# Gating of two batches' dense tiles and one addition moved behind the cluster choice in a two-block AdaLN kernel

## The chip, the cores and the metric

The kernel runs on one core of one Trainium2 chip. The metric is the time of one execution on the device, in microseconds (us). Five engines work side by side and meet through semaphores: TensorE (PE in the profile; its weight loads are PEld), VectorE (DVE), ScalarE (ACT), GpSimd (POOL) and SyncE, whose queue (SPq) issues most of the DMAs.

## What is computed

Two transformer blocks run one after the other on x of 4 batches x 512 rows x 512 columns, in float32. The change lies in the feed-forward part of the first block:

```python
mod = (_silu(L0_c) @ L0_wmod).reshape(4, 6, 1, -1)      # sa, ca, ga, sb, cb, gb
h = _layernorm(x) * (1 + ca) + sa
x = x + ga * attention0(h)
h = _layernorm(x) * (1 + cb) + sb
dots = softmax(h @ centroids.T / 0.1)                    # 64 clusters
hits = dots > 0.01
query_sel = any(hits, axis=1)                            # per row
cluster_sel = any(hits, axis=0)                          # over all 2048 rows
row_sel = cluster_sel[assignments]                       # per output column
dense = h @ weight.T + bias
x = x + gb * where(query_sel[:, None] & row_sel[None, :], dense, 0)
```

`cluster_sel` needs the softmax of all four batches. Only after it is known can an output column be taken or left. The second block (attention with 32 query and 8 key heads, and a gated feed-forward) follows and takes about nine tenths of the time.

## The kernel before

The 2048 rows are 16 tiles of 128 rows, four to a batch. The first block is written out by hand: each engine has one list of steps (`first_tensor`, `first_vector`, `first_scalar`, `first_gpsimd`, `first_sync`), run strictly in that order, with waits on semaphores between engines. So a step that waits holds all that stands behind it on its engine.

The steps around the change, by line:

- `add_outputs(b, tiles)` (L946) adds the attention's result in PSUM (PE's `update`, L1212) to x. `statistics2` and `normal2` (L864 to L907) follow, PE transposes the result (L120), ACT modulates it (L125).
- `cluster_logits(b)` (L957, L958) takes the maximum off the logits that PE's `dots` (L1227) left; ACT's `clusters` (L639) takes the exponential; `cluster_hits(b)` (L962 to L967) makes `qsel`, the row flag, and keeps the largest value of each cluster in `top`.
- `columns2(b)` (L1221), the first product of the logits on PE, waits for the `cluster_logits` of the batch before.
- `whole_linear(t)` (L1242, L1245) is PE's dense product of tile t; ACT's `drain` (L643) copies it to `dense`. POOL (L500) makes the low half of each batch's split input for it.
- `gate_dense(b)` (L814) multiplies the four tiles of a batch by `qsel` and the gate row, in place; `add_rows(b)` (L819) adds x. Batches 0 and 1 get this here; batches 2 and 3 go to DRAM and are done later.
- After `cluster_hits(3)`, `topc` (L1063) is reduced, PE transposes it (L1397), DVE makes `topv` and `selb` (L1065 to L1067), and PE spreads the choice over the columns (L1400). That last product raises `chosen` to `ROWS_SPREAD`. DVE waits for it before `select`, and POOL waits for it before it splits the first weights of the second block (L508, L510, eight instructions of 128x512).
- `select(tiles)` (L822) overwrites x by `dense` where the column is taken. It is done for tiles 0 and 1, then 2 and 3, with the second block's statistics (`spread_of`, `variances_2`, `inverse_2`) between; then come `add_rows(1)`, `select` of tiles 4 to 7, and `whole_chunk`/`low_of` (L1108, L1114), which with POOL's `low_chunk` (L530) make the first operands of the second block's products (L2158).
- PE does the dense tiles 12, 13 and 14 after the spreading, then the transposes of batch 0 (L1411), the dense tile 15, the product for a modulation (L1153), the first key product (L2158), the first query product (L2073), and then waits for the normalised batch 1, `normal_second` (L1137), which it transposes (L120).

Of the kernel before, what the change touches and what calls it, by code (L numbers as in the profile page):

```python
# [29 lines left out]
def adaln_two_blocks(nc, x, Wq, bq, Wk, bk, Wv, bv, ffn_w, ffn_b, cent, assign, c0, wmod0,  # L30
# [26 lines left out]
    with ctx:  # L57
# [152 lines left out]
        with l0:  # L210
# [600 lines left out]
            def gate_row(dve, t):  # L811
                dve.wait_ge(rows_sb, 2 * B)
                dve.wait_ge(drained, t + 1)
                return nc.vector.scalar_tensor_tensor(rows(dense, t), rows(dense, t), qsel[:, t:t + 1], gb_rows[:, t // TB, :],  # L814
                                                      ALU.mult, ALU.mult)

            def add_row(t):

                return nc.vector.tensor_tensor(rows(dense, t), rows(dense, t), rows(X, t), ALU.add)  # L819
# [46 lines left out]
            def variances_2(dve, tiles, done):  # L866
                for t in tiles:
                    last = nc.vector.bn_aggr(mv_2[:, t, :], stats[:, t, :])
                link_vector(dve, last)
                v = slice(tiles[0], tiles[-1] + 1)  # L870
                nc.vector.tensor_scalar(mv_2[:, v, 1], mv_2[:, v, 1], EPS, None, ALU.add).then_inc(done, 1)

            def first_vector(dve):
                def link(ins):
                    link_vector(dve, ins)
# [66 lines left out]
                def add_outputs(b, tiles=range(TB)):  # L942
                    for r in tiles:
                        t = TB * b + r
                        dve.wait_ge(upd_ps, t + 1)
                        nc.vector.tensor_tensor(rows(X, t), rows(X, t), ps[:, BANK_U + t % 2, :], ALU.add).then_inc(x1_done, 1)  # L946
# [7 lines left out]
                def cluster_logits(b):  # L954
                    dve.wait_ge(lgps, b + 1)
                    lp = ps[:, BANK_M, 0:TB * NCL].rearrange("p (t k) -> p t k", t=TB)
                    link(nc.vector.tensor_reduce(cred[:, 0], lp, AX.X, ALU.max))  # L957
                    nc.vector.tensor_tensor(lg[:], lp, wide_c(cred[:, 0]), ALU.subtract).then_inc(lg_done, 1)  # L958

                def cluster_hits(b):  # L960
                    dve.wait_ge(exps_done, b + 1)
                    link(nc.vector.tensor_reduce(cred[:, 1], lg[:], AX.X, ALU.add))  # L962
                    link(nc.vector.reciprocal(cred[:, 1], cred[:, 1]))
                    link(nc.vector.tensor_tensor(pr[:], lg[:], wide_c(cred[:, 1]), ALU.mult))
                    link(nc.vector.tensor_reduce(cred[:, 2], pr[:], AX.X, ALU.max))
                    link(nc.vector.tensor_scalar(qsel[:, tiles_of(b)], cred[:, 2], THRESHOLD, None, ALU.is_gt))
                    link(nc.vector.tensor_tensor(top[:], pr[:] if b == 0 else top[:], pr[:], ALU.max))  # L967

                def gate_dense(b):
                    for t in range(TB * b, TB * (b + 1)):  # L970
                        last = gate_row(dve, t)
                    link(last)

                def add_rows(b):
                    for t in range(TB * b, TB * (b + 1)):
                        last = add_row(t)
                    link(last)
# [68 lines left out]
                normal2(2)  # L1046
                cluster_hits(0)
                add_outputs(3, range(2))
                gate_dense(0)
                add_outputs(3, range(2, 3))  # L1050
                cluster_logits(1)
                add_outputs(3, range(3, 4))
# [2 lines left out]
                cluster_hits(1)  # L1055
                one_hot()
                cluster_logits(2)
                gate_dense(1)
                add_rows(0)
                cluster_hits(2)  # L1060
                cluster_logits(3)
                cluster_hits(3)
# [2 lines left out]
                link(nc.vector.tensor_reduce(topv[:, 0:1], ps[0:NCL, BANK_M, 0:P], AX.X, ALU.max))  # L1065
                link(nc.vector.tensor_scalar(topv[:, 1:2], topv[:, 0:1], THRESHOLD, None, ALU.is_gt))
                nc.vector.tensor_scalar(selb[:], ones[:], topv[:, 1:2], None, ALU.mult).then_inc(chosen, 1)  # L1067
                dve.wait_ge(chosen, ROWS_SPREAD)

                def select(tiles):  # L1070
                    for t in tiles:
                        select_row(t, ps[:, BANK_P, :])
                    dve.wait_ge(x2_done, tiles[-1] + 1)
# [6 lines left out]
                def inverse_2(step, tiles):  # L1080
                    v = slice(tiles[0], tiles[-1] + 1)
                    dve.wait_ge(std_2, step + 1)
                    link(nc.vector.reciprocal(rstd_2[:, v], rstd_2[:, v]))
                    nc.vector.scalar_tensor_tensor(shift[:, v], mv_2[:, v, 0], -1.0, rstd_2[:, v], ALU.mult, ALU.mult) \
                        .then_inc(rstd_done, 1)
# [7 lines left out]
                spread_of(HALVES[1])  # L1093
                variances_2(dve, HALVES[1], var_2)
                inverse_2(1, HALVES[1])
                add_rows(1)
                select(range(TB, TB + 2))
                select(range(TB + 2, 2 * TB))
# [334 lines left out]
        with a:  # L1433
# [41 lines left out]
            with at:  # L1475
# [177 lines left out]
                with nc.Block() as block:  # L1653
# [902 lines left out]
                    @block.vector  # L2556
                    def _(dve):
                        first_vector(dve)

                        dve.sem_inc(o_ready, 1)  # L2560
# [358 lines left out]
```

## Time and profile before

| | us |
|---|---|
| median of 3 runs | 1852.1 |
| lowest, highest | 1851.37, 1853.2 |
| the profiled execution | 1854.24 |
| its span on the core | 1852.5 |
| PE busy in it | 1807.5 |
| DVE busy in it | 1283.4 |
| POOL busy in it | 448.1 |

The profiled execution is 2.1 us longer than the median, and 1.7 us of it lie outside the span. A timeline row gives the start, the length of the group, engine, line, operation, output and inputs, shapes and the count; in brackets stands how long the engine had been idle before it, and what released it. First starts and lengths are in us from the span's start. The last length in a row can reach a little into the next row, since the engines pipeline.

### The profile page before, as it was taken

To read this page: it belongs to the slowest core of one execution; us is meant where nothing else is said; L and a number is where in the kernel's file an instruction comes from. 1 tells how busy PE (TensorE), PEld (TensorE's weight loads), DVE (VectorE), ACT (ScalarE), POOL (GpSimd) and SP (SyncE) were. 2 spreads that over 40 slices of the span, in tenths; PEclk is the share of its full clock that TensorE was granted. 3 is DMA by queue.
4 is the path that set the end of the run, shared out by engine and by line. 5 is a ranking of instruction groups with operands and counts; after the bars stand their busy time and mean duration, and the time that the engine had idled before them with its cause. 6 is when DMAs were issued, how large, how long until landed. Compare 5 with 4: busy or idle time off the path is not lost.

```text
span 1852.5 us, 29061 instructions
## 1 busy us (share of the span) xinstructions
PE 1807.5 (98%) x8863; PEld 1508.2 (81%) x8863; DVE 1283.4 (69%) x3032; ACT 1123.1 (61%) x2620; POOL 448.1 (24%) x429
## 2 busy tenths in 40 slices
PE   6998999999999999999999999999999989999999
PEld 4566788888888888888888888888888867888887
DVE  6897677877767676766777777777777785544442
ACT  5755766667667676766666676666666673333331
POOL 2234404041323224041612123140313132010000
PEclk9899999999999999999999999999999999999999
DMA  9026567666766776776776778677777767313010
GB/s 347 2 80 224 157 191 216 203 192 191 204 200 194 211 200 198 205 231 207 214 211 197 208 202 226 191 217 212 197 213 203 210 186 243 109 57 114 27 41 23
DMA packets 239368, 331.25 MB, mean 179 GB/s; under 512 B 26008, under 2 KB 165528, under 8 KB 238880
## 3 DMA queue, kind: packets, MB, share of 16 engines
q1 hardware_dynamic: 238736, 328.93, 59.6%
q8 instruction: 52, 0.85, 0.2%
q10 hardware_dynamic: 528, 1.05, 0.2%
q14 instruction: 52, 0.43, 0.1%
HBM read 200.39 MB, written 129.50 MB: 178 GB/s over the span
## 4 chain that ended last, share of the span: by engine, by line
PE 79%; DVE 7%; DMA 6%; ACT 4%; SPq 2%; issue 2%; DVEq 0%; ACTq 0%
PE ps L2073 23%; PE ps L2139 15%; PE ps L2264 11%; PE ps L2121 9%; PE ps L2106 9%; PE ps L2246 5%; DMA turned_blocks<-tp 4%; ACT probs L2362 2%; PE ps L2125 1%; PE ps L2103 1%; SPq L1779 1%; PE ps L1245 1%; DMA pd<-turned_blocks 1%; DVE pt L2628 1%; DVE stats L864 1%
## 5 line engine op out<-in xcount | busy, mean ns | idle before, releaser
L2073 PE MATMUL ps<-hA,wq 128*128 128x512 f32 x1536 | 385.8, 400 | 0.0
L2139 PE MATMUL ps<-wo,oT 128*128 128x512 f32 x1536 | 367.2, 390 | 3.7 <-issue 2.3
L2139 PEld LDWEIGHTS ps<-wo,oT 128*128 128x128 f32 x1536 | 287.8, 188 | 64.3 <-issue 3.1
L2604 DVE CUSTOM_DVE_ANT_0 ps<-ps,mask 128x512 f32<-128x512 f32 (+3 forms) x512 | 235.8, 523 | 143.5 <-PE ps L2106 142.9
L2381 ACT ACTIVATE pt<-pd 128x1280 fp32r<-128x1280 f32 x128 | 163.0, 1273 | 272.2 <-PE ps L2121 231.3
L2073 PEld LDWEIGHTS ps<-hA,wq 128*128 128x128 f32 x1536 | 279.0, 188 | 56.4 <-issue 0.2
L2362 ACT ACTIVATE probs<-ps,nmax 128x512 f32<-128x512 f32 (+3 forms) x512 | 263.1, 532 | 71.3 <-DVE nmax L2604 71.3
L2370 ACT ACTIVATE probs<-probs,rinv 128x512 f32<-128x512 f32 (+3 forms) x512 | 246.2, 552 | 38.3 <-DVE rinv L2610 38.3
L2121 PE MATMUL ps<-pt,V 128*128 128x512 f32 (+2 forms) x1152 | 253.3, 349 | 11.1 <-DVE pt L2628 10.5
L2121 PEld LDWEIGHTS ps<-pt,V 128*128 128x128 f32 x1152 | 196.2, 190 | 40.3 <-issue 15.3
L2106 PE MATMUL ps<-kT,qT 128*128 128x512 f32 (+2 forms) x1152 | 224.7, 340 | 0.0
L2106 PEld LDWEIGHTS ps<-kT,qT 128*128 128x128 f32 x1152 | 198.9, 189 | 20.2 <-issue 0.2
L2620 DVE STREAM_TRANSPOSE tp<-probs 128x384 f32<-128x384 f32 (+2 forms) x512 | 208.1, 444 | 6.4 <-DMA turned_blocks<-tp 4.7
L2628 DVE TENSOR_TENSOR pt<-pd,pt 128x1280 fp32r<-128x1280 f32 x128 | 193.0, 1508 | 2.5 <-ACT pt L2381 2.5
L2264 PE MATMUL ps<-fT,gw 128*128 128x512 f32 x448 | 110.9, 390 | 1.2 <-DVE dgb L2797 1.2
L2264 PE MATMUL ps<-fT,uw 128*128 128x512 f32 x448 | 110.6, 389 | 0.0
L1931 POOL CAST wk<-wk_in 128x512 fp32r<-128x512 f32 x15 | 9.2, 612 | 414.8 <-PE ps L2073 414.8
L2362 ACT ACTIVATION_READ_ACCUMULATOR probs<-ps,nmax 128x1 f32 x512 | 107.4, 210 | 0.0
L2264 PEld LDWEIGHTS ps<-fT,gw 128*128 128x128 f32 x448 | 83.9, 188 | 18.8 <-DVE dgb L2797 1.4
L2264 PEld LDWEIGHTS ps<-fT,uw 128*128 128x128 f32 x448 | 84.1, 188 | 17.5
L2246 PE MATMUL ps<-dw,hd 128*128 128x512 f32 x420 | 96.2, 390 | 0.1
L2779 DVE SCALAR_TENSOR_TENSOR hid<-ps,usc,sg 128x512 f32<-128x512 f32 x56 | 42.0, 750 | 75.8 <-PE ps L2264 63.8
(256 smaller groups left out, 2602.3 us busy)
## 6 DMA issues: line engine op xcount, KB each, us to landing
turned_blocks<-tp SPq DMA_DIRECT2D x128, 640.0 KB, 3.5
pd<-turned_blocks SPq DMA_DIRECT2D x512, 160.0 KB, 3.3
wq_next<-in_L_attn_w_q_dram SPq DMA_DIRECT2D x16, 1024.0 KB, 6.5
wo_in<-in_L_attn_w_o_dram SPq DMA_DIRECT2D x15, 1024.0 KB, 8.2
turned_weights<-hf_chunk SPq DMA_DIRECT2D x168, 64.0 KB, 2.6
wm<-in_L_wmod_dram SPq DMA_DIRECT2D x4, 2048.0 KB, 13.5
turned_values<-tv SPq DMA_DIRECT2D x32, 256.0 KB, 3.2
xh_m<-turned_weights SPq DMA_DIRECT2D x28, 256.0 KB, 3.7
```

The costliest lines, as they stand in the source:

```text
L2073: last = nc.tensor.matmul(ps[:, bank, :], w[i][:, c, cols], hT[k][:, c, b * S:(b + 1) * S], start=(c == 0 and n == 0), stop=(c == DC - 1 a ...
L2106: last = nc.tensor.matmul(dst, qT[x_][:, u % 2, (i - 1) * P:i * P], kT[y_][:, b, 0:KEYS[i]], start=(k == 0), stop=(k == 2))
L2121: last = nc.tensor.matmul(by_quadrant(ps[:, BANK_O, kt * P:]), V[x_][:, b, kt, :], blocks(pt[y_][:, :, first:end]), start=(n == 0 and k == ...
L2139: last = nc.tensor.matmul(ps[:, bank, :], oT[x_][:, b, h, r * P:(r + 1) * P], wo[y_][:, h, :], start=(h == 0 and n == 0), stop=(h == GQ - ...
L2246: last = nc.tensor.matmul(ps[:, t, :], hd[j][k][:, t * P:(t + 1) * P], ww[j][2][:], start=(j == 0 and k == 0), stop=(j == FC - 1 and k == 1))
L2264: last = nc.tensor.matmul(ps[:, 2 * (j % 2) + k, :], ww[j][k][:, c, :], fT[x_][:, c, :], start=(c == 0 and x_ == 0), stop=(c == DC - 1 and ...
L2362: nc.scalar.activation(pe_[:, PO[i]:PO[i] + KEYS[i]], ps[:, BANK_S + bank, col:col + KEYS[i]], ACT.Exp, bias=nmax[:, u % 2, i:i + 1], scal ...
L2370: nc.scalar.activation(v, v, ACT.Identity, scale=rinv[:, u % 2, i:i + 1]).then_inc(scaled, 1)
L2381: nc.scalar.activation(flat(pt[0][:]), flat(pd[:, u % 2]), ACT.Copy).then_inc(phi_done, 1)
L2604: nc.vector.tensor_tensor_reduce(out=v, in0=v, in1=mask[:, TB * P - KEYS[i]:], scale=-1.0, scalar=3e38, op0=ALU.add, op1=ALU.min, accum_ou ...
L2620: last = nc.vector.transpose(out=to[:, t:t + 3 * whole - 2:3], in_=p[:, 0:whole])
L2628: nc.vector.tensor_tensor(flat(pt[1][:]), flat(pd[:, u % 2]), flat(pt[0][:]).bitcast(F32), ALU.subtract).then_inc(plo_done, 1)
```

## The change

The gating of batch 0 goes from between two additions of batch 3 to behind `selb`, the last DVE step before the choice is spread. The addition of batch 0 goes from before `cluster_hits(2)` to the same place. The gating of batch 1 goes from before `cluster_hits(2)` to before `add_rows(1)`. No instruction is added or taken away, and the other engines' lists stay as they are.

```diff
@@ -1046,7 +1046,6 @@
                 normal2(2)
                 cluster_hits(0)
                 add_outputs(3, range(2))
-                gate_dense(0)
                 add_outputs(3, range(2, 3))
                 cluster_logits(1)
                 add_outputs(3, range(3, 4))
@@ -1055,8 +1054,6 @@
                 cluster_hits(1)
                 one_hot()
                 cluster_logits(2)
-                gate_dense(1)
-                add_rows(0)
                 cluster_hits(2)
                 cluster_logits(3)
                 cluster_hits(3)
@@ -1065,6 +1062,8 @@
                 link(nc.vector.tensor_reduce(topv[:, 0:1], ps[0:NCL, BANK_M, 0:P], AX.X, ALU.max))
                 link(nc.vector.tensor_scalar(topv[:, 1:2], topv[:, 0:1], THRESHOLD, None, ALU.is_gt))
                 nc.vector.tensor_scalar(selb[:], ones[:], topv[:, 1:2], None, ALU.mult).then_inc(chosen, 1)
+                gate_dense(0)
+                add_rows(0)
                 dve.wait_ge(chosen, ROWS_SPREAD)
 
                 def select(tiles):
@@ -1093,6 +1092,7 @@
                 spread_of(HALVES[1])
                 variances_2(dve, HALVES[1], var_2)
                 inverse_2(1, HALVES[1])
+                gate_dense(1)
                 add_rows(1)
                 select(range(TB, TB + 2))
                 select(range(TB + 2, 2 * TB))
```

## Rows read from the trace of the kernel before

**Rows 1.** The page: PE's busy line, and the chain's shares by engine.
```profile
PE 1807.5 (98%) x8863; PEld 1508.2 (81%) x8863; DVE 1283.4 (69%) x3032; ACT 1123.1 (61%) x2620; POOL 448.1 (24%) x429
PE 79%; DVE 7%; DMA 6%; ACT 4%; SPq 2%; issue 2%; DVEq 0%; ACTq 0%
```

**Rows 2.** Chain that ended last, in order of time, 90 to 230: start, us, what.
```profile
145.32 2.00 PE ps L1400 x2
...
170.57 3.36 DVE xh L1137 x4
```

**Rows 3.** Timeline of DVE, 95 to 200 us.
```profile
110.35 5.81 DVE L814 SCALAR_TENSOR_TENSOR dense<-dense,qsel,gb_rows 128x512 f32<-128x512 f32 x4
116.19 0.69 DVE L946 TENSOR_TENSOR X<-X,ps 128x512 f32<-128x512 f32 x1
...
121.88 1.92 DVE L907 TENSOR_SCALAR xh<-X,mv,rstd 128x512 f32<-128x512 f32 x4
...
132.71 2.50 DVE L819 TENSOR_TENSOR dense<-dense,X 128x512 f32<-128x512 f32 x4
135.24 0.42 DVE L962 TENSOR_REDUCE cred<-lg 128x4 f32<-128x256 f32 x1
...
137.49 0.42 DVE L957 TENSOR_REDUCE cred<-ps 128x4 f32<-128x256 f32 x1
...
142.62 0.58 DVE L1063 TENSOR_REDUCE topc<-top 128x64 f32<-128x256 f32 x1
...
144.09 0.28 DVE L1067 TENSOR_SCALAR selb<-ones,topv 64x128 f32<-64x128 f32 x1
147.36 1.37 DVE L822 COPY_PREDICATED X<-ps,dense 128x512 f32<-128x512 int32 x2 [3.00 <-PE ps L1400]
...
156.05 0.17 DVE L1083 RECIPROCAL rstd<-rstd 128x2 f32<-128x2 f32 x1 [0.87 <-ACT rstd L772]
...
162.89 1.51 DVE L1108 TENSOR_SCALAR hT<-ps,mod 128x512 f32<-128x512 f32 x2
```

**Rows 4.** Timeline of PE, 84 to 200 us.
```profile
111.73 1.13 PE L1212 MATMUL ps<-G,oT__179 16*128 16x512 f32 x4
...
117.73 1.94 PE L1221 MATMUL ps<-hT,cenT 128*64 128x512 f32 x8 [1.22 <-DVE lg L958]
...
123.85 1.09 PE L120 MATMUL ps<-ident,xh 128*128 128x128 f32 x8 [1.01 <-DVE xh L907]
...
134.59 1.00 PE L1227 MATMUL ps<-same_half,colD 128*128 128x64 f32 x8
...
143.25 0.30 PE L1397 MATMUL ps<-ident,topc 128*64 128x128 f32 x1 [3.03 <-DVE topc L1063]
...
158.08 1.91 PE L1411 MATMUL ps<-ident,xh 128*128 128x128 f32 x16
...
173.97 1.09 PE L120 MATMUL ps<-ident,xh 128*128 128x128 f32 x8 [0.88 <-DVE xh L1137]
```

**Rows 5.** Timeline of ACT, 100 to 200 us: the exponential of batch 2.
```profile
130.72 0.41 ACT L639 ACTIVATE lg<-lg 128x256 f32<-128x256 f32 x1
```

**Rows 6.** Timeline of POOL, 100 to 220 us: first and last of eight splits.
```profile
147.40 0.61 POOL L508 CAST wk<-wk_in 128x512 fp32r<-128x512 f32 x1 [5.10 <-PE ps L1400]
148.09 1.28 POOL L510 TENSOR_TENSOR wk<-wk_in,wk 128x512 fp32r<-128x512 f32 x1
...
153.85 1.30 POOL L510 TENSOR_TENSOR wq<-wq_next,wq 128x512 fp32r<-128x512 f32 x1
```

**Rows 7.** Timelines of DVE and POOL in short windows: single gatings, and POOL's work beside.
```profile
111.01 1.76 DVE L814 SCALAR_TENSOR_TENSOR dense<-dense,qsel,gb_rows 128x512 f32<-128x512 f32 x1
...
131.27 1.40 DVE L814 SCALAR_TENSOR_TENSOR dense<-dense,qsel,gb_rows 128x512 f32<-128x512 f32 x2
...
110.40 1.83 POOL L500 TENSOR_TENSOR hP<-hT,hP 128x512 fp32r<-128x512 f32 x1 [8.40 <-ACT hP L125]
```

**Rows 8.** Windows of 2 us: window, length, busy by engine, granted clock, DMA share, GB/s.
```profile
116.00:118.00 2.00, 0.78 (x5) 0.27 (x5) 1.93 (x5) 0.01 (x1) 0.00 (x0) 1.00 0.76 287
...
146.00:148.00 2.00, 2.00 (x4) 0.65 (x3) 0.64 (x2) 0.00 (x0) 0.60 (x1) 0.50 0.00 0
...
152.00:154.00 2.00, 2.00 (x11) 1.63 (x10) 1.93 (x5) 0.77 (x3) 1.92 (x3) 1.00 0.34 131
```

## The prediction, made before the changed kernel ran

> **What bounds the kernel.** I read the page first. PE is busy for 98% of the span, and the chain that ended last is PE for 79% and DVE for 7% [rows 1]. That is an average: the second block is bound by PE, and nothing there changes. So I read the chain in order of time around the change, and then the timelines of the engines from 100 to 200 us. There the chain runs mostly over DVE, goes to PE for the spreading of the choice at 145.32, and is back on DVE at 170.57 [rows 2]. DVE is hardly idle: from 110 to 174 us it waits 3.00 us for the spreading, 0.87 us for a root on ACT [rows 3], and three times under 0.5 us. PE stands three times for DVE before the spreading, for 1.22, 1.01 and 3.03 us, and at 173.97 it stands for 0.88 us for DVE's normalised batch 1 [rows 4]. From there to 230 us the chain goes on over PE, DVE and ACT without a gap. So what counts is how much earlier or later DVE is at 173.9 us. I follow that difference ("shift", minus is earlier) through the stage.
>
> **What is moved.** Gating of batch 0: 5.81 us. Addition of batch 0: 2.50 us, from 132.71. Gating of batch 1 and that addition together: the stretch before 135.24, some 6.9 us [rows 3]. Nearly 12.7 us leave DVE's list before the choice, and DVE's own wait behind it, 3.00 us, is the only hole into which they could go.
>
> **How long a gating takes.** The second gating in the old place took 1.76 us; two later ones took 1.40 us together, 0.70 each [rows 7]. The difference is POOL. Its two-input operation of 128x512 began at 110.40 and took 1.83 us [rows 7], where the same kind takes 1.28 us when it has the time for itself [rows 6]. The times fit two engines that take turns for whole instructions: DVE's first gating to 111.0, POOL to 112.2, DVE to 112.8, and so on. The Trainium skill, "SBUF — State Buffer", says so: VectorE and GpSimd share a port pair, it is an exclusive lock, and the loser is blocked for the whole instruction. The trace agrees (1.76 against 0.70 us). That rule of the Trainium skill speaks against the new place, since POOL's splits start while DVE's moved work runs; with turns it gives the sum below, without them the first rival's.
>
> **Step 1, until the topc reduction.** Without gating 0, DVE is free at 110.4 rather than 116.19. But the next addition needs the third update of batch 3, and PE makes its two from 111.73 to 112.86 [rows 4], so the third is there at about 112.3. Shift of DVE: 112.35 - 116.19 = -3.84; 1.9 us become idle. PE's waits of 1.22 and 1.01 us go: the logits come at about 113.8 and the normalised rows at 123.80 - 3.84 = 119.96 [rows 3], before PE asks for them. Shift of PE: -2.23. The exponential of batch 2 stands on ACT behind the modulation of PE's transposes, so it takes PE's shift: 131.13 - 2.23 = 128.90 [rows 5]. DVE, with gating 1 and addition 0 gone, has been waiting there since 124.5, and `cluster_hits(2)` starts at 128.94 rather than 135.24 [rows 3]. It ends at 131.2, and then DVE waits for PE's logits of batch 3: 134.59 + 1.00 - 2.23 = 133.36 [rows 4]. `cluster_logits(3)` starts at 133.42 rather than 137.49 [rows 3]: shift -4.07. From there to topc all steps hang on each other and on ACT, and POOL's last two low halves lie beside them as before. topc ends at 139.13 rather than 143.20. Of the 12.7 us freed, 4.1 have come through; 8.5 us have turned into idle time (1.9 + 4.4 + 2.2), and the rest is the time that the old gatings lost to POOL's turns.
>
> **Step 2, the spreading.** PE is ready at 140.22 - 2.23 = 138.0 and stands 1.2 us for topc instead of 3.03. The half clock matters here: with 3.03 us of standing the granted clock went to 0.50, that is 1.2 of 2.4 GHz, and it was back at 1.00 by 152; with 1.22 us of standing, at 117, it stayed at 1.00 [rows 8]. I take full clock for the new kernel. selb is ready at 144.37 - 4.07 = 140.30. The rest of tile 11 runs to 140.8, and the spreading, 2.00 us at half clock [rows 2], takes about 1.0: it ends at 141.8 rather than 147.3.
>
> **Step 3, gating 0 and addition 0.** DVE starts at 140.35. Three gatings of 0.66 us (the start-to-start distance in the pair of 1.40 us) reach 142.4. POOL's splits are released at 141.9 and from then on the two take turns: five DVE instructions are left (one gating, four additions, 0.6 each), and before each goes one of POOL's, in the order cast, subtraction, cast, subtraction, cast... as it lists them: 0.55 (cast) or 1.25 (subtraction) each [rows 6]. 142.4 + 5 x 0.6 + 3 x 0.55 + 2 x 1.25 = 149.55; without turns it would be 140.35 + 4 x 0.66 + 2.50 = 145.5. No row shows a cast against a two-input DVE operation from the DVE side; its price lies between 0 and 0.61 us, and I take 0.55, since the subtraction held DVE for its full length. `select` starts at 149.55 rather than 147.36: shift +2.2. DVE does not wait for the spreading any more. Behind it POOL is nearly through its splits, so two small DVE operations that were stretched before (together some 0.3 us on the path) run free: shift +1.9 at 156.05.
>
> **Step 4, gating 1.** It stands on the path: 4 x 0.66 = 2.65 us. POOL has nothing to do then (its splits end at 152.8, and its next operation needs DVE), so there are no turns. The wait of 0.87 us [rows 3] lies before the place of gating 1 and hides nothing of it. Bounds: 2.6 us alone and 4.4 us with the turns of the old place. Shift at `whole_chunk`: 162.89 + 1.9 + 2.65 = 167.4, that is +4.5. What follows on DVE, POOL and ACT up to the normalised batch 1 hangs on this.
>
> **Step 5, PE meanwhile.** PE has the dense tiles 12 to 14 done at about 151.5 instead of 158.2, and then stands until ACT has drained tile 13 behind its own normalisation, about 157.8, and for the second half of the rows until 159.9. So PE loses its lead, and some 6 us of standing should bring the half clock again, as 3.03 us did. Its transposes and tile 15 then end at about 167.3 instead of 163, if all run at half clock; the first operand for L2158 comes at 169.6. So this lies beside DVE's path, with about 1 us to spare after tile 15's drain and the modulation product. The shift at 173.97 is DVE's: +4.5.
>
> **DMAs and queues.** SyncE's spill of dense tile 13 and the load behind it move by about +1.9 us, the stores of tiles 4 to 7 by +4.5, behind the same waits as before; nothing in the list overtakes. Their data are wanted only 20 us later.
>
> **Sum.** -4.1 (choice earlier) - 3.0 (DVE's wait filled) + 5.2 (gating 0 and addition 0 alone) + 4.1 (turns with POOL) - 0.3 + 2.65 (gating 1) = +4.5 us. Against the profiled execution, 1854.24 + 4.5 = 1858.7; that one lay 2.1 us over the median, so I forecast 1852.1 + 4.5 = 1856.6.
>
> **Rivals.**
> 1. *Few turns.* POOL's splits start late, or DVE keeps the port through its queued additions. Then step 3 ends between 145.5 and 147.6 and the shift is +0.5 to +2.6: 1852.6 to 1854.7. For it: POOL's first operation let DVE's first gating pass at its full speed of 0.75 us. Against it: the second took 1.76 us [rows 7]. A spreading at half clock (end 143.3) would also bring it, since gating 0 is then over when POOL starts. Chance 0.22.
> 2. *PE becomes the bound through the clock.* After step 5's standing the half clock lasts beyond tile 15. It decides if it still holds at 171 us: the first key product (3.3 us at full clock) and the first query product (2.9) would then each cost up to as much again, against 0.88 us of slack at 173.97 [rows 4]. Shift +6 to +9: 1858 to 1861. Against it: after the stand of 3.03 us the clock was back by 152 [rows 8], and tile 15 gives PE unbroken work before L2158. Chance 0.12.
> 3. *Faster: PE, not DVE, sets the stage's end.* The 0.88 us before 173.97 and DVE's chain behind 156 would have to be slack, for instance because the releaser is inferred wrongly and the path goes over PE's products and their drains. Then the stands saved count and the moved gatings do not: -(1.22 + 1.01 + 1.84) = -4.1, so 1848.0. It decides if PE's own work is what ends last at 174; the DVE rows, with no hole behind `inverse_2`, speak against it. Chance 0.06.
> 4. *Nothing to see.* A later wait in the second block's first units, such as those on the DMAs of the transposed blocks, takes up the shift: 1852.1, within 1 us. Against it: the chain has no idle there. Chance 0.07.
>
> **How the numbers follow.** The forecast has 0.53, with its own range from 1854.9 (a cast that holds nobody, or one turn less) to 1858.8 (gating 1 with turns, one turn more). About 0.2% is what a measurement of this kernel can tell from no change, here 3.7 us, so the border is at 1855.8. Some 0.14 of the forecast's 0.53 lie below it. Slower: 0.39 + 0.12 and a little of rival 1, 0.53. Same: 0.14 + 0.20 + 0.07 = 0.41. Faster: 0.06. Range: from rival 1's lower end less half a microsecond of noise, 1852.0, to the middle of rival 2, 1860.0.
>
> **What would show it.** Right: the third addition of batch 3 at 112.3; idle before `cluster_hits(2)` and `cluster_logits(3)` of some 4.4 and 2.2 us; topc done at 139.1; PE idle 1.2 us before L1397, clock at 1.00 after it; no idle on DVE before `select`; additions of batch 0 at 1.1 to 1.9 us each; gating 1 at 0.7 us each; a long stand of PE before L1411; and PE's L120 at about 178.5 behind DVE's L1137. Wrong: a topc later than 141, which would mean that the exponentials do not follow PE; additions at 0.69 us beside POOL's splits (rival 1); L2158 or L2073 at half clock around 171 us (rival 2); PE's L120 at 174 or before (rivals 3 and 4).

## The result, and the profile after

| | before | after |
|---|---|---|
| median of 6 runs each, us | 1851.75 | 1860.51 |
| lowest, highest | 1849.24, 1853.42 | 1859.28, 1864.49 |
| the profiled execution | 1854.24 | 1863.24 |
| its span | 1852.5 | 1861.5 |

The ratio is 1.0047, 95% interval 1.0035 to 1.0058: slower by 8.8 us, where 4.5 was forecast, and 0.5 us beyond the range. Three later comparisons, of five rounds each, gave 3.3, 3.7 and 4.8 us (below).

The page after, to set beside [rows 1]: busy time by engine, and the chain's shares.

```profile
PE 1813.2 (97%) x8863; PEld 1512.1 (81%) x8863; DVE 1279.4 (69%) x3032; ACT 1122.5 (60%) x2620; POOL 448.2 (24%) x429
PE 81%; DMA 7%; DVE 5%; ACT 4%; SPq 2%; issue 1%; POOL 0%; DVEq 0%; ACTq 0%
```

PE is busy for 5.7 us more with as many instructions, and DVE for 4.0 us less. Neither says what the change costs; that is in the timelines.

DVE after, for [rows 3]:

```profile
114.79 0.69 DVE L946 TENSOR_TENSOR X<-X,ps 128x512 f32<-128x512 f32 x1 [2.47 <-PE ps L1212]
...
130.57 0.42 DVE L962 TENSOR_REDUCE cred<-lg 128x4 f32<-128x256 f32 x1 [3.56 <-ACT lg L639]
...
135.10 0.42 DVE L957 TENSOR_REDUCE cred<-ps 128x4 f32<-128x256 f32 x1 [2.33 <-PE ps L1227]
...
140.27 0.58 DVE L1060 TENSOR_REDUCE topc<-top 128x64 f32<-128x256 f32 x1
...
141.95 2.72 DVE L814 SCALAR_TENSOR_TENSOR dense<-dense,qsel,gb_rows 128x512 f32<-128x512 f32 x4
144.71 5.40 DVE L819 TENSOR_TENSOR dense<-dense,X 128x512 f32<-128x512 f32 x4
150.14 1.37 DVE L822 COPY_PREDICATED X<-ps,dense 128x512 f32<-128x512 int32 x2
...
158.17 0.17 DVE L1082 RECIPROCAL rstd<-rstd 128x2 f32<-128x2 f32 x1 [0.96 <-ACT rstd L772]
...
167.73 1.51 DVE L1108 TENSOR_SCALAR hT<-ps,mod 128x512 f32<-128x512 f32 x2
```

PE after, for [rows 4]:

```profile
113.63 1.13 PE L1212 MATMUL ps<-G,oT__179 16*128 16x512 f32 x4
...
140.91 0.30 PE L1397 MATMUL ps<-ident,topc 128*64 128x128 f32 x1 [1.28 <-DVE topc L1060]
...
142.54 1.12 PE L1400 MATMUL ps<-asg,selb 64*128 64x512 f32 x2
...
158.15 3.97 PE L1411 MATMUL ps<-ident,xh 128*128 128x128 f32 x16 [5.42 <-ACT dense L643]
...
178.61 1.09 PE L120 MATMUL ps<-ident,xh 128*128 128x128 f32 x8
```

Three holes of 2.47, 3.56 and 2.33 us stand on DVE where the moved work had been. The moved work now stands before `select`, with no idle ahead of it, and the four additions take 5.40 us where they had taken 2.50 [rows 3].

**A common zero.** The group of L1212 that starts at 113.63 here starts at 111.73 in [rows 4]. PE's work up to it is the same in both kernels and waits for nothing that was moved, so these 1.9 us are not the change. From here on I measure each trace from the start of that group to the start of PE's L120 for batch 1, the last row above: 62.24 us before, 64.98 after, so +2.74 us. I call this the stage. Of the 9.0 us between the two spans, 1.9 lie before the stage, 2.7 in it, and 4.4 behind it, where both kernels run the same instructions.

### The profile page after: what moved, and what is told of

Same layout as the page of the kernel before. It is cut to its first block, busy times and chain, and to the rows that moved or that the text cites. A ratio compares the mean times of both kernels' runs of the same rounds, so it can differ in the third digit from the quotient of the medians.

```text
span 1861.5 us, 29060 instructions
## 1 busy us (share of the span) xinstructions
PE 1813.2 (97%) x8863; PEld 1512.1 (81%) x8863; DVE 1279.4 (69%) x3032; ACT 1122.5 (60%) x2620; POOL 448.2 (24%) x429
## 4 chain that ended last, share of the span: by engine, by line
PE 81%; DMA 7%; DVE 5%; ACT 4%; SPq 2%; issue 1%; POOL 0%; DVEq 0%; ACTq 0%
PE ps L2073 23%; PE ps L2139 15%; PE ps L2264 11%; PE ps L2121 9%; PE ps L2106 9%; PE ps L2246 5%; DMA turned_blocks<-tp 5%; ACT probs L2362 2%; PE ps L1245 2%; PE ps L2125 1%; SPq L1779 1%; PE ps L2103 1%; PE ps L120 1%; DVE pt L2628 1%; PE ps L1212 1%
## 5 line engine op out<-in xcount | busy, mean ns | idle before, releaser
L2073 PE MATMUL ps<-hA,wq 128*128 128x512 f32 x1536 | 385.9, 400 | 0.0
L2073 PEld LDWEIGHTS ps<-hA,wq 128*128 128x128 f32 x1536 | 279.1, 188 | 56.4 <-issue 0.2
L2121 PE MATMUL ps<-pt,V 128*128 128x512 f32 (+2 forms) x1152 | 253.4, 349 | 11.8 <-DVE pt L2628 11.4
L2121 PEld LDWEIGHTS ps<-pt,V 128*128 128x128 f32 x1152 | 196.1, 190 | 41.9 <-issue 17.0
```

The source lines that it names most:

```text
L2073: last = nc.tensor.matmul(ps[:, bank, :], w[i][:, c, cols], hT[k][:, c, b * S:(b + 1) * S], start=(c == 0 and n == 0), stop=(c == DC - 1 a ...
L2121: last = nc.tensor.matmul(by_quadrant(ps[:, BANK_O, kt * P:]), V[x_][:, b, kt, :], blocks(pt[y_][:, :, first:end]), start=(n == 0 and k == ...
```

## The experiments

The stage in every trace, in us; the runs are told one by one below. "Choice" is the end of `topc`, counted from the zero; "to select" goes from there to the start of the first `select`; "rest" goes from the first L2121, which follows the stage's end by 29.5 to 29.8 us in all of them, to the last instruction. The last column is the difference of medians, against runs of the kernel before on the same chip.

| trace | zero at | choice | to select | stage | rest | timed |
|---|---|---|---|---|---|---|
| before | 111.73 | 31.47 | 4.16 | 62.24 | 1648.9 | |
| ctl | 115.34 | 31.45 | 2.84 | 60.72 | 1646.6 | -0.4 |
| ctl2 | 109.22 | 31.57 | 4.49 | 62.26 | 1650.6 | +0.8 |
| warm_b | 111.49 | 31.62 | 2.84 | 60.70 | 1648.6 | -2.3 |
| after | 113.63 | 27.22 | 9.29 | 64.98 | 1653.4 | +8.8 |
| rep | 116.38 | 27.23 | 9.28 | 66.75 | 1646.8 | +3.3 |
| rep2 | 111.67 | 27.23 | 9.28 | 65.17 | 1648.9 | +3.7 |
| rep3 | 110.27 | 27.23 | 9.28 | 65.02 | 1647.3 | +4.8 |
| b0 | 113.79 | 27.23 | 9.28 | 62.72 | 1652.2 | -0.4 |
| g1 | 111.34 | 29.72 | 2.84 | 61.74 | 1648.3 | +0.2 |
| noturn | 111.87 | 27.23 | 6.38 | 62.53 | 1643.7 | +1.0 |
| warm | 115.71 | 27.23 | 9.29 | 65.22 | 1649.1 | +5.5 |
| pockets | 111.36 | 27.48 | 2.91 | 59.80 | 1650.9 | -3.3 |
| pockets2 | 111.25 | 27.23 | 2.91 | 57.99 | 1648.7 | -2.7 |

The runs come in three groups, each on one chip: ctl, rep, b0, g1; rep2, noturn, warm, pockets; ctl2, rep3, pockets2, warm_b.

### The changed kernel again (rep, rep2, rep3)

The kernel is unchanged. Theory: the stage gives some 3 to 4.5 us, and what the first result had above it belongs to executions and not to the change. Rival: the whole 8.8 us belong to the change.

> The changed kernel once more. In its first trace PE's transposes of batch 1 come 4.64 us later than before, 1.90 of them already there at 109 us, ahead of any edit, and the span is 9.0 us longer. Theory A: the stage from 109 to 179 us gives +2.7 us again (within 0.3), the rest changes place and size, and the timed difference comes nearer to +3 to +6. Theory B: +8 to +9 again, with slips near 62, 746, 1000 and 1500 us.

> The changed kernel a third time, for the size of the difference (+8.8 us, then +3.3 us). From the traces so far the edited stage, from PE's third update of batch 3 to its transposes of batch 1, costs 2.7 to 4.5 us, the rest is what executions differ by. If so: +3 to +6 us timed. If the first measurement was right, +8 to +9.

> The changed kernel a fourth time. The same stretch on DVE takes 65.1 us again (64.93, 65.12, 65.11 so far), so 2.9 to 4.4 us more than in the kernel before, and the time is 3 to 6 us over it. If +8.8 us was the true size, +8 to +9; then the two measurements between would have been the odd ones.

Measured: 1.0020 [1.0002, 1.0037], 1.0023 [1.0008, 1.0038], 1.0032 [1.0021, 1.0043]. None of the three reaches 1.0047. All four intervals hold only 1.0035 to 1.0037 in common, some 6.6 us; the three later ones have 1.0021 to 1.0037. So the first comparison stands apart, at the edge of what the others allow.

In one of the four traces, rep, PE ends the stage late. PE of rep; in after the second half of L2158 and L2073 took 2.39 and 2.91 us:

```profile
172.78 1.95 PE L2158 MATMUL ps<-hA,wk 128*128 128x512 f32 x6 [2.11 <-POOL hA L530]
175.31 2.93 PE L2158 MATMUL ps<-hA,wk 128*128 128x512 f32 x6 [0.58 <-POOL hA L530]
178.03 4.17 PE L2073 MATMUL ps<-hA,wq 128*128 128x512 f32 x12
...
183.13 1.10 PE L120 MATMUL ps<-ident,xh 128*128 128x128 f32 x8
```

DVE of rep:

```profile
178.16 3.34 DVE L1137 TENSOR_SCALAR xh<-X,mv,rstd 128x512 f32<-128x512 f32 x4
```

Windows of rep (length, busy by engine, granted clock, DMA share, GB/s):

```profile
170.00:172.00 2.00, 0.67 (x8) 0.00 (x0) 2.00 (x3) 0.60 (x1) 0.63 (x1) 1.00 0.97 343
...
178.00:180.00 2.00, 2.00 (x6) 1.60 (x5) 1.96 (x3) 1.04 (x3) 1.92 (x3) 0.50 0.94 248
```

DVE has the normalised rows at 181.5 and PE comes to them at 183.13, 1.6 us late, with its clock at 1.2 of 2.4 GHz. That is the outcome of rival 2, in one trace of four, but not by its road. The rival has the half clock of the long stand last on beyond tile 15. In rep the clock was back at 1.00 from 170 to 172 us, and it fell a second time after a second stand, 2.11 us before the first half of L2158, for POOL's operand. The other three traces have this stand and a shorter second half clock too. PE of after:

```profile
170.01 2.29 PE L2158 MATMUL ps<-hA,wk 128*128 128x512 f32 x6 [2.29 <-POOL hA L530]
```

In rep2 and rep3, with stands of 2.54 and 2.81 us there, PE still waits 0.42 and 0.53 us for DVE at L120, against 0.88 us in [rows 4]. In after it waits for nothing: its own work ends at 178.6, when DVE's rows are ready, so the two paths come out level.

### The kernel before again, and its clock (ctl, ctl2, warm_b)

ctl and ctl2 are the kernel before, unchanged. warm_b keeps PE at work ahead of its stand of 3.03 us:

```diff
+    pe.wait_ge(x1_done, NT)
+    for _ in range(12):
+        nc.tensor.matmul(ps[:, BANK_U, :], ones_p[:], bias_p[:], start=True, stop=True)
     pe.wait_ge(chosen, TOP_FOUND)
```

> The kernel before, unchanged, as a yardstick for what one execution's trace differs from the next. Theory A (the changed kernel's time outside the changed stage is chance): within 1.5 us of the kernel before in the timed rounds, but its trace differs from the first trace of before by 1 to 3 us in places that no edit touches: the first 60 us, where the changed kernel was already 1.93 us late, and single slips of 0.5 to 1.5 us in the second block's groups, of which the changed kernel showed +0.8 at 746 us, +2.0 from 990 to 1004 us and +1.5 from 1485 to 1508 us. Theory B (those slips belong to the change): this trace lies within 0.5 us of the first one all along.

> The kernel before once more. From PE's third update of batch 3 to the end of DVE's normalised batch 1 the first trace took 62.2 us, with the half clock behind the stand of 3.03 us, the second 60.7, with the clock at 1.00. This one is one or the other, not between. Timed within 1.5 us of the kernel before.

> The kernel before, with 12 products without use on PE (their results are overwritten) where it stands 3.03 us for topc. If that stand is what brings the half clock at 144 us, the clock stays at 1.00 through the spreading, DVE waits 1.67 us for it and never 3.00, and the stretch takes 60.7 us. By how much the mean falls says how often the kernel before pays: between 0 and 1.5 us.

Measured: 0.9992 [0.9980, 1.0005], 1.0003 [0.9993, 1.0013], 0.9989 [0.9977, 1.0002]. The median of warm_b lies 2.3 us lower, but its interval takes in no change. The first `select` waits for the spreading in all of them. DVE of ctl, of ctl2, and of warm_b:

```profile
149.63 1.38 DVE L822 COPY_PREDICATED X<-ps,dense 128x512 f32<-128x512 int32 x2 [1.67 <-PE ps L1400]
```
```profile
145.28 1.35 DVE L822 COPY_PREDICATED X<-ps,dense 128x512 f32<-128x512 int32 x2 [3.31 <-PE ps L1400]
```
```profile
145.95 1.38 DVE L822 COPY_PREDICATED X<-ps,dense 128x512 f32<-128x512 int32 x2 [1.67 <-PE ps L1403]
```

PE of ctl, a window of ctl, and PE of ctl2:

```profile
146.85 0.30 PE L1397 MATMUL ps<-ident,topc 128*64 128x128 f32 x1 [3.02 <-DVE topc L1063]
148.48 1.12 PE L1400 MATMUL ps<-asg,selb 64*128 64x512 f32 x2
```
```profile
148.00:150.00 2.00, 2.00 (x7) 0.84 (x6) 0.36 (x1) 0.00 (x0) 0.33 (x1) 1.00 0.00 0
```
```profile
140.85 0.30 PE L1397 MATMUL ps<-ident,topc 128*64 128x128 f32 x1 [3.01 <-DVE topc L1063]
```

In ctl PE stands for 3.02 us, as long as before, but its clock stays at 2.4 GHz and L1400 takes 1.12 us instead of 2.00 [rows 2]. The wait is then 1.67 us, and the stage 60.72 rather than 62.24. Of the three traces of the kernel before, two have the half clock here and one has not; warm_b, where PE is kept at work, has not either. So the 3.00 us of [rows 3] was not the wait of the kernel but one of its two values. Against the stage at full clock the change costs 4.3 us, and against the one at half clock 2.7.

### Each part alone (b0, g1)

b0 moves gating and addition of batch 0 only; g1 moves gating 1 only.

```diff
# b0, from before
-                gate_dense(0)          # between the additions of batch 3
-                add_rows(0)            # before cluster_hits(2); gate_dense(1) stays there
+                gate_dense(0)          # behind selb
+                add_rows(0)
# g1, from before
-                gate_dense(1)          # before cluster_hits(2); add_rows(0) stays there
+                gate_dense(1)          # behind inverse_2(1, HALVES[1])
```

> Only the gating and the addition of batch 0 are moved behind the choice; the gating of batch 1 stays in its old place. By DVE's path: the choice comes as early as in the changed kernel (topc 4.1 to 4.3 us earlier than before, measured from the same point ahead of the edits), the additions take turns with the splits on POOL, select starts 0.9 us later than before, and the stage ends at 0 to +0.4 us. Time: within 1.5 us of the kernel before. If instead the moved work at the choice carries most of the +8.8 us, it is at least +5 us.

> Only the gating of batch 1 is moved, to before the addition of batch 1. By DVE's path: topc 1.8 us earlier (bound by the logits of batch 3 on PE), the wait for it on PE 1.1 us instead of 3.03, so the full clock stays and the spreading ends 3.2 us earlier; then +2.7 us for the gating alone on the path: stage -0.6 us, time within 1.5 us of the kernel before. If the gating in front of the addition of batch 1 carries most of the +8.8 us, it is at least +5 us.

Measured: b0 0.9991 [0.9976, 1.0006], g1 1.0001 [0.9987, 1.0015]. Neither costs anything that the timing tells, though together they cost some 4 us. The stages do not settle it either: 62.72 and 61.74 us lie between 0.5 us below and 2.0 us above the two values of the kernel before. DVE of b0, then of g1:

```profile
127.08 4.36 DVE L814 SCALAR_TENSOR_TENSOR dense<-dense,qsel,gb_rows 128x512 f32<-128x512 f32 x4
...
144.87 5.40 DVE L819 TENSOR_TENSOR dense<-dense,X 128x512 f32<-128x512 f32 x4
150.30 1.37 DVE L822 COPY_PREDICATED X<-ps,dense 128x512 f32<-128x512 int32 x2
```
```profile
127.91 4.23 DVE L819 TENSOR_TENSOR dense<-dense,X 128x512 f32<-128x512 f32 x4
...
135.29 0.42 DVE L957 TENSOR_REDUCE cred<-ps 128x4 f32<-128x256 f32 x1 [0.91 <-PE ps L1227]
...
143.90 1.38 DVE L822 COPY_PREDICATED X<-ps,dense 128x512 f32<-128x512 int32 x2 [1.67 <-PE ps L1400]
...
152.72 2.74 DVE L814 SCALAR_TENSOR_TENSOR dense<-dense,qsel,gb_rows 128x512 f32<-128x512 f32 x4
```

b0 has its choice as early as after (27.23): gating 1 fits whole into the wait before `cluster_hits(2)` and costs nothing there. Taking it out as well, as the change does, earns nothing and adds 2.3 us of stage (64.98 - 62.72 for after, 2.29 for rep3). In g1 the choice comes 1.8 us earlier than before and not 4.2. The addition of batch 0, left in its old place, takes POOL's turns there (4.23 us for 2.50 us of work), but that is not the reason: DVE still waits 0.91 us behind it for PE's logits of batch 3. PE begins them 22.85 us after the zero, as before (22.86), since gating 0 is still in its old place and PE still stands 1.21 and 0.97 us for DVE.

### The turns with POOL (noturn)

The changed kernel, with POOL's splits held back until the first `select` operation is done:

```diff
+    pool.wait_ge(x2_done, 1)
     split(wk, wk_in, slice(0, HD), 0, wk_split)
```

> The changed kernel, with POOL's splits held until DVE's first select is done, so that nothing of POOL's lies beside the moved gatings and additions. If POOL's turns stretch the additions, they take 2.50 us instead of 5.40 and select and the stage's end come 2.9 us earlier than in the changed kernel (the stage 62 to 63 us long instead of 65 to 67.5); timed 2 to 3 us less. If something else stretches them (the semaphore chain, the place), they stay at 5.4 us. Against it: POOL's later splits could hold the first key product; they would end near 157, 12 us before it needs them.

Measured: 1.0006 [0.9990, 1.0022], 2.7 us less than rep2 in the same group, though the two intervals overlap. DVE of noturn, then its POOL:

```profile
140.19 2.73 DVE L815 SCALAR_TENSOR_TENSOR dense<-dense,qsel,gb_rows 128x512 f32<-128x512 f32 x4
142.95 2.50 DVE L820 TENSOR_TENSOR dense<-dense,X 128x512 f32<-128x512 f32 x4
145.48 1.36 DVE L823 COPY_PREDICATED X<-ps,dense 128x512 f32<-128x512 int32 x2
```
```profile
146.38 0.61 POOL L508 CAST wk<-wk_in 128x512 fp32r<-128x512 f32 x1 [8.19 <-DVE X L823]
```

The additions take 2.50 instead of 5.40 us, and the way to `select` 6.38 instead of 9.28. So the turns are worth 2.90 us, and 2.5 of them arrive at the end of the stage (62.53 against 65.0 in after and rep3). POOL of after, where it takes its turns:

```profile
143.73 1.42 POOL L508 CAST wk<-wk_in 128x512 fp32r<-128x512 f32 x1 [3.77 <-PE ps L1400]
145.23 1.61 POOL L510 TENSOR_TENSOR wk<-wk_in,wk 128x512 fp32r<-128x512 f32 x1
146.79 1.08 POOL L508 CAST wq<-wq_next 128x512 fp32r<-128x512 f32 x1
147.94 1.62 POOL L510 TENSOR_TENSOR wq<-wq_next,wq 128x512 fp32r<-128x512 f32 x1
```

The first cast, 0.61 us of work, ran until 145.15, 0.48 us after the last gating had ended. It had begun during the third, and the fourth still went ahead of it. From there on it is one for one: four of POOL's instructions, among four additions. Both kinds are stretched, the casts too. noturn shows what the turns cost; the order in them is read from these times.

### PE's half clock before L1411 (warm)

The changed kernel, with PE kept at work in its long stand:

```diff
     whole_linear(14)
+    for _ in range(20):
+        nc.tensor.matmul(ps[:, BANK_M, :], ones_p[:], bias_p[:], start=True, stop=True)
 ...
+    for _ in range(8):                 # before make_mod(pe, 8)
+        nc.tensor.matmul(ps[:, 7, :], ones_p[:], bias_p[:], start=True, stop=True)
```

> The changed kernel, with work without use on PE where it stood: 20 products of 128x512 behind dense tile 14 and 8 in front of the first modulation product of the second block (their results are overwritten). If the half clock that follows the stand of 5.4 us reaches the path, as the second trace of the changed kernel suggests (half clock over the first key and query products), the clock stays at 1.00 from 145 to 185 us and the stage is as long as DVE's path alone asks, 64.5 to 65.2 us, never 66 to 67.5. If the half clock is beside the path, nothing changes in the stage. In no case does it explain more than 2 us.

Measured: 1.0024 [1.0011, 1.0037], as rep2's 1.0023 in the same group. One window of after and the same of warm, then a later one of warm:

```profile
158.00:160.00 2.00, 1.85 (x8) 1.57 (x8) 1.79 (x5) 1.57 (x5) 0.00 (x0) 0.50 0.69 262
```
```profile
158.00:160.00 2.00, 1.35 (x6) 0.77 (x5) 1.28 (x5) 2.00 (x4) 0.00 (x0) 1.00 0.13 49
...
170.00:172.00 2.00, 2.00 (x10) 0.83 (x3) 1.97 (x3) 0.60 (x1) 1.27 (x1) 0.50 0.97 275
```

The half clock over L1411 and tile 15 is gone, and the stage stays as it was, 65.22 us: that work lies beside DVE's path. But the clock did not stay at 1.00 until 185 us, as was expected: after a stand of 3.04 us before L1153 it was at half once more, over the added products, and back before L2158. So what the second half clock costs, the one that made PE late in rep, is read from rep and pockets alone.

### The same work in the holes (pockets, pockets2)

If only what fits into a wait is free, the twelve instructions should be placed by the size of the holes. From the kernel before (pockets and pockets2 are the same kernel; `gates` and `adds` do single tiles):

```diff
                 add_outputs(3, range(2))
-                gate_dense(0)
+                gates((0, 1))
 ...
-                gate_dense(1)
-                add_rows(0)
+                gates((2, 3))
                 cluster_hits(2)
+                adds((0, 1, 2))
                 cluster_logits(3)
 ...             # behind selb
+                adds((3,))
+                gates((4,))
 ...
+                gates((5,))
                 inverse_2(1, HALVES[1])
+                gates((6, 7))
                 add_rows(1)
```

> The same twelve instructions laid into the waits that the changed kernel's trace shows on DVE: gatings 0 and 1 where DVE waits 2.46 us for the update, 2 and 3 in the 3.56 us before the hits of batch 2, additions 0 to 2 in the 2.32 us before the logits of batch 3, addition 3 and gating 4 in the 1.67 us before the spreading is done, gating 5 in the 0.96 us for the root; only gatings 6 and 7 (1.3 us) stay on the path. If the waits are free room, topc comes 4 us earlier than before, select too, and the stage is 58.5 to 60 us long against 60.9 to 62.2 in the kernel before and 65 to 67.5 in the changed one: time 1.5 to 3 us under before. If POOL's turns fill the same room, the gain shrinks to zero.

> The laid-out version again, for its size (first -3.3 us). The stretch on DVE takes 58.0 us again. Timed 2 to 4 us under the kernel before.

Measured: 0.9982 [0.9966, 0.9997] and 0.9985 [0.9970, 0.9999], that is 3.3 and 2.7 us faster than the kernel before, and 7.0 and 7.5 us faster than the changed one in the same groups. Both intervals end close below 1. DVE of pockets2:

```profile
109.86 2.43 DVE L814 SCALAR_TENSOR_TENSOR dense<-dense,qsel,gb_rows 128x512 f32<-128x512 f32 x2
112.48 0.69 DVE L946 TENSOR_TENSOR X<-X,ps 128x512 f32<-128x512 f32 x1 [0.19 <-PE ps L1226]
...
124.61 3.03 DVE L814 SCALAR_TENSOR_TENSOR dense<-dense,qsel,gb_rows 128x512 f32<-128x512 f32 x2
128.26 0.42 DVE L962 TENSOR_REDUCE cred<-lg 128x4 f32<-128x256 f32 x1 [0.62 <-ACT lg L639]
...
130.50 1.89 DVE L819 TENSOR_TENSOR dense<-dense,X 128x512 f32<-128x512 f32 x3
132.72 0.42 DVE L957 TENSOR_REDUCE cred<-ps 128x4 f32<-128x256 f32 x1 [0.33 <-PE ps L1241]
...
141.39 1.38 DVE L822 COPY_PREDICATED X<-ps,dense 128x512 f32<-128x512 int32 x2 [0.36 <-PE ps L1414]
```

The holes of 2.47, 3.56 and 2.33 us have shrunk to 0.19, 0.62 and 0.33, and the wait for the spreading, 1.67 us at full clock, to 0.36, while the choice comes as early as in after (27.23; 27.48 in pockets). In the trace of pockets, PE again had its clock at half over the first key and query products, after a stand of 2.27 us, and ended the stage 1.8 us late; in that of pockets2 the half clock was over before the query product, and PE waited 0.29 us for DVE.

## Why the prediction was right or wrong, step by step

**Step 1, right.** The choice came 4.25 us earlier (27.22 against 31.47); 4.07 was forecast. The idle times of 2.47, 3.56 and 2.33 us were forecast as 1.9, 4.4 and 2.2, for the reasons given: PE's update, ACT's exponential, PE's logits. The addition behind the update began 1.16 us after the zero, where the working had about 0.6; that moved 0.6 us from the second hole to the first. Of the work moved, about two thirds bought nothing; b0 shows this from the other side. The working puts the rest of the 12.7 us, which is 0.1, down to POOL's turns. That reading is wrong: at 0.66 us for a gating, the turns are some 4.9 us of the 12.7, and they are part of what the 4.1 and 8.5 us add up to. And the waits under 0.5 us are four, not three (0.27, 0.48, 0.39 and 0.27), which changes nothing.

**Step 2, right.** PE stood for 1.28 us, the clock stayed at full speed, and L1400 took 1.12 us.

**Step 3, right in kind, too large by 1.1 us.** From `topc` to `select` the sum gave 149.55 - 139.13 = 10.42 us and the trace 9.29. The term that failed is the 4.1 us of turns, which measured 2.9. "Five DVE instructions are left" was one too many, since POOL's first cast waited for the last gating: 0.55 us. The other 0.7 us is the prices: four turns at 0.55 and 1.25 us are 3.6. The Trainium skill, "SBUF — State Buffer", section "SBUF: two separate sides", has an exclusive lock held for the whole instruction; additions at 5.40 us with POOL's splits beside them and at 2.50 us without agree with it. Rival 1 had step 3 end by 147.6 at the latest; `select` came at 148.24 on the scale of [rows 3]. It was right that DVE's queued gatings went ahead of POOL, and wrong for the additions. Behind `select` the root's reciprocal (158.17, before 156.05) lies 0.22 us later on the common scale, against +1.9 forecast: 1.3 of this is carried over from `select` (+0.9 there, forecast +2.2), and the rest is a gain of 0.66 us, forecast as 0.3, where POOL had stretched DVE's work before.

**Step 4, right.** Gating 1 cost 2.74 us, forecast 2.65, alone on the path, and `whole_chunk` moved from +0.2 to +2.9 us.

**Step 5, right in its result in after, rep2 and rep3.** PE stood for 5.42 us, its clock went to half, and it did not end later than DVE; warm shows that this half clock cost nothing. The working missed the second stand, of 2.1 to 2.8 us before L2158, and the half clock behind it. That took up PE's slack in after and made it 1.6 us late in rep. So rival 2's outcome came once in four traces through a fall that it did not foresee. Rival 3 is out, since the stage grew with DVE's path. Rival 4 is not borne out: the first L2121 carries the whole shift, and the later comparisons still show 3.3 to 4.8 us.

**The sum.** +4.5 us was forecast and the stage gave +2.7 against [rows 3]: the shift at `select` was 1.3 us smaller, and the gain behind it 0.4 us larger. A second slip was in the base: "DVE's wait filled, -3.0" is 1.3 us less in a trace whose clock does not fall, which makes the change cost 4.3 us. I took one execution's clock for the kernel's. Three comparisons gave 3.3 to 4.8 us, between the one and the other or just above. That they lie so near the +4.5 is partly luck, since the turns were sized too high and DVE's wait was taken at its longer value.

**What failed is the range.** The step that failed is the term for all that lies outside the stage: "half a microsecond of noise", taken off at the lower end only. The upper end is called the middle of rival 2, which would be 1859.5 and not 1860.0, and has nothing for noise. The traces show far more. The zero lies between 109.2 and 116.4 us with the same instructions ahead of it, and "rest" between 1643.7 and 1653.4 with the same instructions in it. The windows of ctl and of before on the way to the zero:

```profile
50.00:60.00 10.00, 10.00 (x44) 5.12 (x40) 7.04 (x19) 5.80 (x8) 2.45 (x3) 0.50 0.01 2
```
```profile
50.00:60.00 10.00, 8.46 (x57) 5.28 (x57) 8.77 (x25) 8.75 (x16) 1.95 (x3) 0.83 0.01 2
```

Here ctl has PE at 1.2 GHz throughout and finishes 44 products, and before has 0.83 of full speed and finishes 57; their zeros are 3.6 us apart. The 9 to 12 executions of one kernel in a set spread over 8 to 14 us in ten of the twelve later sets. By my estimate from that, a median of six can be off by a few us, and the range should have allowed for it.

**What stays open.** In the trace of after, 4.4 us lie behind the stage, in small slips at about 746, 990 to 1004, and 1485 to 1508 us. Both traces of the unchanged kernel have such slips against before: ctl one of about 1.5 us the other way and ctl2 one of about 2 us the same way, both between 960 and 1020 us. So they come without any change.

That all six first runs lay 8.8 us up, and no later set did, is not explained by this. One number on record goes with it: the mean granted clock of each execution. It was 0.985 to 0.988 in all six, and above 0.988 in 26 of the 35 later executions of the same kernel. The eight of the 35 with 0.985 to 0.988 took 1861.3 us in the mean, as the first six did (1861.2); the 26 others took 1855.5. So the first runs look like the slow part of the later ones. Whether the lower clock made them longer, or other waits did both, is not shown, nor why all six fell there.

## What to carry to other kernels

Work taken out of a busy engine's list ahead of a critical result helps only until the next input of that engine is late: count the time freed against each following wait. Here 12.7 us moved away brought 4.2, and putting it behind the result cost 7 in the stage; cut into single instructions and laid into the waits of 2.5, 3.6, 2.3 and 1.7 us, the same work made the kernel about 3 us faster. A wait read from one trace can have two lengths if a clock changes in it, and two medians of a few runs can differ by more than the stage under study, so repeat both kernels before a difference is explained.

## What the runs showed of the hardware

- After a stand of PE of 3.01 or 3.03 us the granted clock fell to half in ctl2 and before, and after 3.02 us it stayed at 2.4 GHz in ctl, with the same instructions. After 1.28 or 1.29 us it stayed in all four traces of the changed kernel, and after 2.11 to 2.81 us before L2158 it fell in all four. The Trainium skill, "TensorE: Matmul & The Clock Gate", section "What's actually happening", has idle time bring the throttle back; these rows agree, and the length of the stand alone did not decide.
- POOL's first instruction (0.61 us of work) took 1.42 us although DVE's gatings were separate instructions: in all four traces of the changed kernel it began during the third of them and ended 0.47 or 0.48 us after the fourth. The one-for-one order came behind it.
- The time to the zero differs by up to 7.2 us among the traces, with the same instructions of PE ahead of it, and goes with the clock granted early on. Where the mean from 30 to 80 us was 0.66 to 0.71 (ctl, warm, rep) the zero lay at 115.3 to 116.4 us; where it was 0.83 (seven traces) at 109.2 to 111.9.
